# Attention: TensorE's step order from a list schedule made at build time instead of a fixed round

## The chip, the cores and the metric

The kernel runs on one core of a Trainium2 chip. The metric is the device time of one execution in microseconds (us). The kernel computes two transformer-like layers in one launch. The first layer's attention is a stage of its own inside it, and the change touches that stage alone.

## The reference, cut to what matters

The attention stage has 2 batches of 2048 tokens, 16 heads of 16 columns each, a causal mask and a key mask (`T` is 2048 here, `H` 16, `dh` 16):

```python
Qh = Q.reshape(B, T, H, dh)
Kh = K.reshape(B, T, H, dh)
Vh = V.reshape(B, T, H, dh)
scores = jnp.einsum('bqhd,bkhd->bhqk', Qh, Kh) / np.sqrt(dh)
scores = jnp.where(key_mask[:, None, None, :] == 0, NEG, scores)
tril = jnp.tril(jnp.ones((T, T), dtype=scores.dtype))
scores = jnp.where(tril[None, None, :, :] == 0, NEG, scores)
attn = jax.nn.softmax(scores, axis=-1)
attn = attn * query_mask[:, None, :, None]
out = jnp.einsum('bhqk,bkhd->bqhd', attn, Vh).reshape(B, T, U)
```

## The kernel before, in words

`two_layers` runs its stages one behind the other; `attention` is the second. The 32 head-and-batch pairs go through it in 8 head quads of 4 heads (`NQ`, `HQ`). For each quad the softmax is made in two passes. A first pass computes the scores with queries on the partitions, only to find each row's maximum. A second pass computes the scores again, with keys on the partitions and the negated maximum added inside the matmul, so that ScalarE can take the exponential straight away and the values matmul can use it without a transpose.

All engines walk one list, `steps`, made by `plan()` at build time; each takes the entries that concern it, in the order of the list. The kinds are:

- **first** (640, 80 a quad): two matmuls side by side (64x128 tiles, L993) write the scores of two heads for one query tile and up to 512 keys into one of the two slots of `pf`. VectorE reduces them to maxima `mx`: with one TENSOR_REDUCE (L1159) when the block is off the diagonal (48 a quad), with two masked reductions (L1155) when it ends on it (32 a quad). The slot is free after that; `free_slot` waits for it.
- **max** (192): one of six small VectorE steps per block of 512 queries (L1165 to L1177) that split the negated maximum into three bf16 parts, `msp`.
- **rows** (32, one for each quad and query block): TensorE transposes `msp` into a `pf` slot (L999), VectorE copies it to `mT` (L1182), and SyncE sends it by four DMAs (L870) into rows of the operand `qa`. Score steps of that block wait for it (`rows_in`).
- **score** (1152, 144 a quad): for one head, up to 512 queries and one or two key tiles, one or two matmuls (128x128 tiles, L1012), with a mask matmul on the diagonal (L1016), write one of three buffers of `pst` (`NS`). ScalarE takes the exponential into `prob` (L1051) and so frees the buffer.
- **values** (288, 36 a quad): the matmuls of one group for four heads (128x32 tiles, L1028), with `prob` of the group's four exponentials as moving operand. There are three `prob` buffers (`NP`).
- **take** and **turn** (32 each): at the end of a query block VectorE copies `po` to `osb` (L1187), TensorE transposes it into a `pf` slot (L1037), and VectorE divides by the row sums into `att` (L1195 to L1202).

The old `plan()` is a fixed round. For every group it puts four score steps, then the values step of the group `LAG` = 2 groups back, then a turn if one is due. Ahead of each score step it puts as many first steps as keep the first pass `lead(s)` of a quad ahead of the second pass (at most 0.52 of a quad), going by column counts. After each first step it puts one to three max steps, and the rows step comes once six more steps have been listed after the split. It knows no times.

SyncE's queue follows the list too: the rows steps' DMAs, and the loads of quad n+2 (17 DMAs) where the list has quad n's last values step. GpSimd waits for each quad's last values step (L925), stores `att`, and at quad 5 begins sums for the next stage, on which VectorE works (`ahead`) among the scores that follow the last first, max or rows step.

Of the kernel before, what the change touches and what calls it, by code (L numbers as in the profile page):

```python
# [16 lines left out]
P = 128  # L17
# [650 lines left out]
def attention(nc, qs_dram, ks_dram, vs_dram, kbias_dram, mask_dram, att_dram, slots_dram, x_dram, xn_dram, ffn_dram, gamma, x1_dram,  # L668
# [11 lines left out]
    HQ = 4  # L680
    NQ = B * HEADS // HQ
# [6 lines left out]
    W1 = 512  # L688
    NS = 3


    first = []
# [5 lines left out]
    groups = []  # L698
# [7 lines left out]
    NG, N1 = len(groups), len(first)  # L706
    ends = [i for i, f in enumerate(first) if f[2] + f[3] == (f[1] + 1) * P]
    last = [max(g for g in range(NG) if groups[g][0] == qb) for qb in range(NB)]

    LAG, NP = 2, 3
    assert NG % NP == 0
    cost1 = [f[3] + 64 for f in first]
    width = [sum(p[2] for p in g[1]) + 64 for g in groups]
    done_at = [max(i for i, f in enumerate(first) if f[1] // 4 == qb) for qb in range(NB)]

    def lead(s):  # L720
        return min(0.52, 0.21 + 0.6 * s)

    def plan():
        steps, done, spent, passed, chain_, waiting = [], 0, 0.0, 0.0, [], []

        def chain_step():
            if chain_:
                k, m, qb = chain_.pop(0)
                steps.append(("max", m, qb, k))
                if k == 5:  # L730
                    waiting.append((len(steps), m, qb))

        def first_steps(due):
            nonlocal done, spent
            while done < NQ * N1 and spent + cost1[done % N1] / sum(cost1) / 2 <= due:
                m, i = divmod(done, N1)
                steps.append(("first", m, i, 0))
                spent += cost1[i] / sum(cost1)
                done += 1
                chain_step()  # L740
                chain_step()
                if i in done_at:
                    chain_.extend((k, m, done_at.index(i)) for k in range(6))
                    chain_step()

        for j in range(NQ * NG + LAG + 1):
            n, g = divmod(j, NG)
            for hh in range(HQ):
                if n < NQ:
                    first_steps(passed + lead(passed))  # L750
                if waiting and (len(steps) >= waiting[0][0] + 6 or n == NQ):
                    _, m, qb = waiting.pop(0)
                    steps.append(("rows", m, qb, 0))
                if done == NQ * N1:
                    chain_step()
                if n < NQ:
                    steps.append(("score", n, g, hh))
                    passed += width[g] / sum(width) / HQ
            if LAG <= j < NQ * NG + LAG:
                vn, vg = divmod(j - LAG, NG)  # L760
                steps.append(("values", vn, vg, 0))
                if vg in last:
                    steps.append(("take", vn, last.index(vg), 0))
            if j >= LAG + 1:
                tn, tg = divmod(j - LAG - 1, NG)
                if tg in last:
                    steps.append(("turn", tn, last.index(tg), 0))
        assert done == NQ * N1 and not waiting and not chain_
        return steps

    steps = plan()


# [23 lines left out]
    part = sb("c_part", [P, NQB, TT, C // NQB])  # L797
# [1872 lines left out]
def two_layers(nc, x, Wq, bq, Wk, bk, Wv, bv, gamma, beta, Wr, br, W1, b1, W2, b2, w_qkv, w_proj, router_wT, e_bias,  # L2670
# [31 lines left out]
    with ExitStack() as kept:  # L2702
# [3 lines left out]
        with nc.cleanup_on_exit():  # L2706
            with ExitStack() as first:
                shared, load = first_weights(nc, w, beta, C, Wr.shape[1], first)
                with ExitStack() as c:
                    norm_and_project(nc, flat(x), xn, mask, kbias, w, shared, load, QT, qs, ks, vs, ffn, B, T, C, HEADS, HV, c)  # L2710
            with ExitStack() as c:
                attention(nc, rows(qs), rows(ks), vs, kbias, mask, att, slots, flat(x), xn, ffn, gamma, x1, ahead, ahead_r,
                          B, T, C, HEADS, HV, c)
# [79 lines left out]
```

## Time and profile before

| | us |
|---|---|
| median of 3 runs | 2173.13 (2168.01 to 2175.15) |
| profiled execution | 2178.65 |
| its span | 2176.2 |

| engine | busy us | share of the span |
|---|---|---|
| TensorE matmul (PE) | 1814.4 | 83% |
| TensorE weight load (PEld) | 944.1 | 43% |
| VectorE (DVE) | 1514.0 | 70% |
| ScalarE (ACT) | 1031.5 | 47% |
| GpSimd (POOL) | 536.8 | 25% |

The profile is of one execution. A busy time is the sum in which an engine has an instruction under way; matmuls overlap, since the next one streams while the last one drains, so the distance from start to start tells more than the duration. In the rows a timeline line gives the start, the duration of the merged run, the engine, line and operation, and in brackets how long the engine was idle before it and what released it. SPq is the queue on which SyncE issues DMAs.

### The profile page before, as it was taken

What the parts mean: (1) busy time and instruction counts of PE and PEld (TensorE: products, weight loads), DVE (VectorE), ACT (ScalarE), POOL (GpSimd) and SP (SyncE); (2) the same over time, 40 slices, a digit from 0 to 9 for tenths busy, and PEclk for the clock granted to TensorE, in tenths of its full rate; (3) what the DMA queues carried; (4) which work ended last, traced back from release to release, by engine and by line L of the source; (5) the groups of instructions that cost most, each with busy time, mean ns of one, the idle gap of its engine ahead of it and who ended that gap; (6) DMA issues with size and microseconds to landing.
All of it is one profiled execution on the core that took longest, in us unless ns stands there. A gap on an engine that the chain in (4) does not pass through costs nothing. (4 is left out here: it accounts for less than half of the span.)

```text
span 2176.2 us, 34165 instructions
## 1 busy us (share of the span) xinstructions
PE 1814.4 (83%) x11999; PEld 944.1 (43%) x11999; DVE 1514.0 (70%) x3496; ACT 1031.5 (47%) x1908; POOL 536.8 (25%) x592
## 2 busy tenths in 40 slices
PE   0898926899999999999899959799327788999998
PEld 0565602222222222222223236555317555888865
DVE  7987656888888888888788845378206896444456
ACT  3554403466667666666566825356001444323210
POOL 1443350000000000000340000100650786566620
PEclk9999958999999999999999989999658899999999
DMA  3466563013030404040620163000420622566556
GB/s 97 140 212 220 187 157 69 1 25 127 12 140 3 148 2 150 2 150 2 227 79 11 40 230 128 18 2 1 158 85 9 214 95 94 175 188 187 185 198 222
DMA packets 158712, 238.67 MB, mean 110 GB/s; under 512 B 19762, under 2 KB 127282, under 8 KB 156882
## 3 DMA queue, kind: packets, MB, share of 16 engines
q1 hardware_dynamic: 122706, 152.46, 23.0%
q0 software_dynamic: 23136, 75.65, 9.5%
q10 hardware_dynamic: 12704, 8.39, 1.2%
q8 instruction: 99, 1.62, 0.3%
q14 instruction: 67, 0.55, 0.1%
HBM read 116.23 MB, written 119.82 MB: 108 GB/s over the span
## 5 line engine op out<-in xcount | busy, mean ns | idle before, releaser
L1051 ACT ACTIVATE c_prob<-c_pst 128x512 f32<-128x512 f32 (+1 forms) x1152 | 603.1, 573 | 362.3 <-PE c_pst L1012 221.5
L1159 DVE TENSOR_REDUCE c_mx<-c_pf 128x2 f32<-128x1024 f32 x384 | 463.0, 1223 | 92.3 <-PE c_pf L993 89.4
L1012 PE MATMUL c_pst<-c_qa,c_ka 128*128 128x512 bf16 (+3 forms) x1280 | 393.9, 358 | 38.2 <-DMA c_qa<-c_mT 34.6
L993 PE MATMUL c_pf<-c_ka,c_qa 64*128 64x512 bf16 (+3 forms) x1280 | 234.9, 364 | 79.2 <-DVE c_mx L1159 26.4
L1028 PE MATMUL c_po<-c_prob,c_vh 128*32 128x512 f32 (+3 forms) x2560 | 297.2, 547 | 1.5 <-DVE c_osb L1187 0.5
L1155 DVE CUSTOM_DVE_ANT_0 c_spare<-c_pf,c_cut 128x384 f32<-128x384 f32 (+3 forms) x512 | 231.1, 492 | 51.0 <-PE c_pf L993 46.3
L1012 PEld LDWEIGHTS c_pst<-c_qa,c_ka 128*128 128x128 bf16 x1280 | 108.6, 97 | 284.4 <-ACT c_prob L1051 122.7
L993 PEld LDWEIGHTS c_pf<-c_ka,c_qa 64*128 64x128 bf16 x1280 | 61.9, 93 | 313.0 <-issue 126.5
L925 POOL IOTA c_zero<- 128x24 int32 x6 | 1.3, 215 | 697.4 <-PE c_po L1028 697.4
L1980 POOL DMA_INDIRECT s_parts<-x_yr,x_tags x144 | 141.0, 979 | 85.8 <-DVE x_yr L2635 62.4
L2519 PE MATMUL x_ps<-x_gu,x_xs 128*128 x576 | 137.6, 382 | 0.0
L1980 POOL DMA_INDIRECT s_slots<-x_rows,place x128 | 125.8, 983 | 37.9 <-issue 31.3
L2620 DVE TENSOR_TENSOR x_h<-x_ps,x_sg 128x256 f32<-128x256 f32 x72 | 30.6, 424 | 142.4 <-ACT x_sg L2589 123.5
L2067 PE MATMUL i_pm<-i_X,i_AQ 64*64 64x64 f32 x768 | 41.9, 248 | 82.7 <-issue 70.3
L2519 PEld LDWEIGHTS x_ps<-x_gu,x_xs 128*128 128x128 f32 x576 | 105.0, 192 | 11.5
L1016 PE MATMUL c_pst<-c_negk,c_idb 128*128 128x128 bf16 x512 | 95.7, 220 | 0.0
L1028 PEld LDWEIGHTS c_po<-c_prob,c_vh 128*32 128x32 f32 x2560 | 54.6, 109 | 86.4 <-issue 43.2
L2582 ACT COPY x_xs<-x_ps 128x512 f32<-128x512 f32 x72 | 42.2, 587 | 84.5 <-issue 61.3
L2067 PEld LDWEIGHTS i_pm<-i_X,i_AQ 64*64 64x64 f32 x768 | 35.9, 159 | 88.3 <-issue 75.2
L2540 PE MATMUL x_ps<-x_d,x_hT 128*128 x288 | 74.1, 380 | 0.1
L365 POOL TENSOR_TENSOR b_parts<-b_r,b_parts 128x512 bf16<-128x512 f32 x32 | 57.6, 1819 | 57.7 <-ACT b_parts L502 57.7
L2335 ACT ACTIVATE k_e<-k_d 128x1024 f32<-128x1024 f32 x32 | 33.9, 1060 | 74.0 <-POOL k_en L2271 50.5
(383 smaller groups left out, 2934.9 us busy)
## 6 DMA issues: line engine op xcount, KB each, us to landing
s_slots<-c_zero POOLq DMA_DIRECT2D x6, 3264.0 KB, 19.9
x_xr<-s_slots SPq DMA_DIRECT2D x72, 272.0 KB
x_rows<-s_parts SPq DMA_DIRECT2D x8, 2048.0 KB, 8.8
c_qa<-s_qs SPq DMA_DIRECT2D x64, 192.0 KB, 8.3
c_ka<-s_ks SPq DMA_DIRECT2D x64, 192.0 KB, 9.0
s_qs<-b_parts SPq DMA_DIRECT2D x32, 256.0 KB, 2.4
s_ks<-b_parts SPq DMA_DIRECT2D x32, 256.0 KB, 2.7
s_vs<-b_va SPq DMA_DIRECT2D x32, 256.0 KB, 3.8
```

Of the source, the lines that this page charges most:

```text
L365: nc.gpsimd.tensor_tensor(parts[:, i, 2, :], r[:, i, :], parts[:, i, 1, :], ALU.subtract).then_inc(parts_ok, 1)
L993: mm = nc.tensor.matmul(pf[:, slot, h - fh, 0:kn], qa[r, s, h, qt * P:(qt + 1) * P], ka[r, s, h, k0:k0 + kn], start=True, stop=True, tile_ ...
L1012: mm = nc.tensor.matmul(pst[:, u % NS, at:at + qn], ka[:, s, hh, kt * P:(kt + 1) * P], qa[:, s, hh, qb * QB + q0:qb * QB + q0 + qn], start ...
L1016: mm = nc.tensor.matmul(pst[:, u % NS, at:at + P], idb[:], negk[:], start=False, stop=True)
L1028: mm = nc.tensor.matmul(po[HV * h:HV * h + HV, q0:q0 + qn], vh[:, s, kt, h, :], prob[:, a % NP, h, at:at + qn], start=(kt == 0), stop=(a i ...
L1051: nc.scalar.activation(prob[:, g % NP, hh, 0:w], pst[:, u % NS, 0:w], ACT.Exp).then_inc(exp_ok, 1)
L1155: ins = nc.vector.tensor_tensor_reduce(spare[:, h, 0:kn], pf[:, slot, h, 0:kn], cut[:, W1 - kn:], 1.0, 0.0, ALU.add, ALU.max, mx[:, fh + h ...
L1159: nc.vector.tensor_reduce(mx[:, fh:fh + 2, qt, part], pf[:, slot, :, 0:kn], AX.X, ALU.max).then_inc(max_ok, 1)
L1980: return nc.gpsimd.indirect_dma_start(out=dst, out_offset=bass.IndirectOffsetOnAxis(ap=index.bitcast(U32), axis=0), in_=src, in_offset=None)
L2067: mm = nc.tensor.matmul(out[h, s % 2 * NG + g, k, 0:width], lhs(h, n), rhs(h, n), start=True, stop=True, tile_position=(h.start, h.start))
L2519: mm = nc.tensor.matmul(pgu[:, m % 2, i, :], xs[:, m % 2, i, k, :], gu[:, k, bass.ds(e, 1), :].rearrange("p o n -> p (o n)"), start=(k == ...
L2540: mm = nc.tensor.matmul(pyr[:, m % 2, i, :], hT[:, m % 2, i, :], d[:, bass.ds(e, 1), :].rearrange("p o n -> p (o n)"), start=True, stop=True)
```

## The change

`plan()` no longer follows a fixed round. It keeps a clock for TensorE, VectorE and ScalarE, with costs in microseconds for each step, and picks again and again, among the kinds that may come next (first, score, values, rows, turn), the one that can begin earliest. A step of another kind than the one before it begins `SWITCH` = 0.1 later. Each kind has a small bonus or malus (`prefer`). First steps may come only while the first pass is within `lead` of the second, now up to 0.67 of a quad. A score may come only when its rows step is listed and fewer than `NP` groups wait for their values. The steps themselves, their waits and their tiles are the same, and so is all code behind `steps = plan()`.

```diff
--- before.py
+++ after.py
@@ -709,63 +709,130 @@
 
 
 
-    LAG, NP = 2, 3
+    NP, SLOTS = 3, 2
     assert NG % NP == 0
-    cost1 = [f[3] + 64 for f in first]
-    width = [sum(p[2] for p in g[1]) + 64 for g in groups]
+    share1 = [(f[3] + 64) / sum(f[3] + 64 for f in first) for f in first]
+    width = [sum(p[2] for p in g[1]) for g in groups]
+    share2 = [(w + 64) / sum(w + 64 for w in width) / HQ for w in width]
     done_at = [max(i for i, f in enumerate(first) if f[1] // 4 == qb) for qb in range(NB)]
-
-
+    opens = [g for g in range(NG) if g == 0 or groups[g - 1][0] != groups[g][0]]
+
+
+
+    SWITCH, SIGNAL, DRAIN, ROW = 0.1, 0.06, 0.17, 1 / 2400
+    prefer = dict(first=0.11, score=0.0, values=-0.18, rows=0.17, turn=0.29)
 
     def lead(s):
-        return min(0.52, 0.21 + 0.6 * s)
+        return min(0.67, 0.34 + 0.51 * s)
 
     def plan():
-        steps, done, spent, passed, chain_, waiting = [], 0, 0.0, 0.0, [], []
+        steps, chain_, split_, turns = [], [], [], []
+        exp_end, values_end, slot_free, rows_at, taken = [], [], [0.0] * SLOTS, {}, [0.0]
+        pe, shape, act, dve = 0.0, None, 0.0, 0.0
+        firsts = scores = values = 0
+        spent = passed = 0.0
+
+        def start(kind, ready):
+            return max(pe + (SWITCH if kind != shape else 0.0), ready + SIGNAL)
+
+        def issue(kind, ready, stream):
+            nonlocal pe, shape
+            begun = start(kind, ready)
+            pe, shape = begun + stream, kind
+            return pe
+
+        def reduce_at(ready, cost):
+            nonlocal dve
+            dve = max(dve, ready) + cost
+            return dve
 
         def chain_step():
             if chain_:
                 k, m, qb = chain_.pop(0)
                 steps.append(("max", m, qb, k))
+                ready = reduce_at(0.0, 0.19)
                 if k == 5:
-                    waiting.append((len(steps), m, qb))
-
-        def first_steps(due):
-            nonlocal done, spent
-            while done < NQ * N1 and spent + cost1[done % N1] / sum(cost1) / 2 <= due:
-                m, i = divmod(done, N1)
+                    split_.append((ready, m, qb))
+
+        def score_ready():
+            j, hh = divmod(scores, HQ)
+            n, g = divmod(j, NG)
+            if j - values >= NP or (n, groups[g][0]) not in rows_at:
+                return None
+            ready = exp_end[scores - NS] if scores >= NS else 0.0
+            return max(ready, rows_at[n, groups[g][0]]) if hh == 0 and g in opens else ready
+
+        def values_ready():
+            if (values + 1) * HQ > scores or values % NG in last and turns:
+                return None
+            ready = exp_end[(values + 1) * HQ - 1]
+            return max(ready, taken[-1]) if values % NG in opens else ready
+
+        while values < NQ * NG:
+            ready = {"score": score_ready() if scores < NQ * NG * HQ else None, "values": values_ready()}
+            if firsts < NQ * N1 and firsts // N1 <= values // NG + 1 and spent + share1[firsts % N1] / 2 <= passed + lead(passed):
+                ready["first"] = slot_free[-SLOTS]
+            if split_:
+                ready["rows"] = max(split_[0][0], slot_free[-SLOTS])
+            if turns:
+                ready["turn"] = max(turns[0][0], slot_free[-SLOTS])
+            ready = {kind: at for kind, at in ready.items() if at is not None}
+            if not ready:
+                if chain_:
+                    chain_step()
+                    continue
+                ready["first"] = slot_free[-SLOTS]
+            kind = min(ready, key=lambda k: start(k, ready[k]) - prefer[k])
+            at = ready[kind]
+            if kind == "first":
+                m, i = divmod(firsts, N1)
+                fh, qt, k0, kn, part = first[i]
                 steps.append(("first", m, i, 0))
-                spent += cost1[i] / sum(cost1)
-                done += 1
+                end = issue(kind, at, kn * ROW)
+                whole = k0 + kn < (qt + 1) * P
+                slot_free.append(reduce_at(end + DRAIN + 0.043, 1.14 * kn / W1 if whole else 2 * (0.153 + 0.00104 * kn) + 0.02))
+                firsts += 1
+                spent += share1[i]
                 chain_step()
                 chain_step()
                 if i in done_at:
                     chain_.extend((k, m, done_at.index(i)) for k in range(6))
                     chain_step()
-
-        for j in range(NQ * NG + LAG + 1):
-            n, g = divmod(j, NG)
-            for hh in range(HQ):
-                if n < NQ:
-                    first_steps(passed + lead(passed))
-                if waiting and (len(steps) >= waiting[0][0] + 6 or n == NQ):
-                    _, m, qb = waiting.pop(0)
-                    steps.append(("rows", m, qb, 0))
-                if done == NQ * N1:
+            elif kind == "rows":
+                ready_, m, qb = split_.pop(0)
+                steps.append(("rows", m, qb, 0))
+                slot_free.append(reduce_at(issue(kind, at, SIGNAL) + DRAIN, 0.2))
+                rows_at[m, qb] = dve + 7.5
+            elif kind == "turn":
+                ready_, n, a = turns.pop(0)
+                steps.append(("turn", n, a, 0))
+                slot_free.append(reduce_at(issue(kind, at, 0.24) + DRAIN, 1.15))
+            elif kind == "score":
+                if firsts == NQ * N1:
                     chain_step()
-                if n < NQ:
-                    steps.append(("score", n, g, hh))
-                    passed += width[g] / sum(width) / HQ
-            if LAG <= j < NQ * NG + LAG:
-                vn, vg = divmod(j - LAG, NG)
-                steps.append(("values", vn, vg, 0))
-                if vg in last:
-                    steps.append(("take", vn, last.index(vg), 0))
-            if j >= LAG + 1:
-                tn, tg = divmod(j - LAG - 1, NG)
-                if tg in last:
-                    steps.append(("turn", tn, last.index(tg), 0))
-        assert done == NQ * N1 and not waiting and not chain_
+                j, hh = divmod(scores, HQ)
+                n, g = divmod(j, NG)
+                qb, pieces = groups[g]
+                steps.append(("score", n, g, hh))
+                end = issue(kind, at, width[g] * ROW + sum(0.063 if p[0] >= 4 * qb else 0.008 for p in pieces)) + DRAIN + 0.037
+                if hh == 0 and j >= NP:
+                    end = max(end, values_end[j - NP] + SIGNAL)
+                act = max(act, end) + 0.065 + 0.00084 * width[g]
+                exp_end.append(act + 0.1)
+                scores += 1
+                passed += share2[g]
+            else:
+                n, g = divmod(values, NG)
+                steps.append(("values", n, g, 0))
+                values_end.append(issue(kind, at, 4 * width[g] * ROW) + DRAIN)
+                values += 1
+                if g in last:
+                    a = last.index(g)
+                    steps.append(("take", n, a, 0))
+                    taken.append(reduce_at(values_end[-1], 0.6))
+                    turns.append((taken[-1], n, a))
+        steps.extend(("turn", n, a, 0) for ready_, n, a in turns)
+        assert firsts == NQ * N1 and not chain_ and not split_
         return steps
 
     steps = plan()
```

## Rows read from the trace of the kernel before

**Rows 1.** The page, part 1: engine, busy us, share of the span, instructions.
```profile
PE 1814.4 (83%) x11999; PEld 944.1 (43%) x11999; DVE 1514.0 (70%) x3496; ACT 1031.5 (47%) x1908; POOL 536.8 (25%) x592
```

**Rows 2.** Busy us by stretch (instructions): the stage, three steady quads; then granted clock, DMA.
```profile
296.00:1256.00 960.00, 858.29 (x5792) 259.02 (x5791) 796.53 (x1908) 603.11 (x1152) 72.29 (x66) 0.96 0.22 70
706.00:1040.00 334.00, 314.70 (x2173) 96.06 (x2171) 282.62 (x673) 226.09 (x432) 6.54 (x9) 1.00 0.22 74
```

**Rows 3.** Timeline of GpSimd: its IOTA behind quads 0 and 5, the last sum.
```profile
483.19 0.22 POOL L925 IOTA c_zero<- 128x24 int32 x1 [165.09 <-PE c_po L1028]
...
1040.04 0.21 POOL L925 IOTA c_zero<- 128x24 int32 x1 [106.05 <-PE c_po L1028]
...
1118.86 2.36 POOL L945 TENSOR_TENSOR QT<-QT,c_ff 128x1024 f32<-128x1024 f32 x1
```

**Rows 4.** Timeline of TensorE in the steady part, 602 to 606 us.
```profile
602.85 0.64 PE L1028 MATMUL c_po<-c_prob,c_vh 128*32 128x256 f32 x8
603.42 0.39 PE L993 MATMUL c_pf<-c_ka,c_qa 64*128 64x512 bf16 x2
603.74 0.60 PE L1012 MATMUL c_pst<-c_qa,c_ka 128*128 128x512 bf16 x2
604.28 0.39 PE L993 MATMUL c_pf<-c_ka,c_qa 64*128 64x512 bf16 x2
604.60 0.39 PE L1012 MATMUL c_pst<-c_qa,c_ka 128*128 128x512 bf16 x1
```

**Rows 5.** Who waited for whom, 296 to 1256 us: total us, times, longest us.
```profile
PEld c_pf L993 <- DVE c_mx L1159: 101.9, 172, 1.7
...
PE c_pst L1012 <- DMA c_qa<-c_mT: 34.6, 10, 11.3
...
PE c_pf L993 <- DVE c_mx L1159: 26.4, 47, 1.5
```

**Rows 6.** Timeline of TensorE in quad 0: the first two rows steps, and the third score.
```profile
318.74 0.27 PE L999 MATMUL c_pf<-c_idb,c_msp 128*48 128x128 bf16 x1 [0.72 <-DVE c_mx L1159]
324.14 0.59 PE L1012 MATMUL c_pst<-c_qa,c_ka 128*128 128x512 bf16 x1 [5.13 <-DMA c_qa<-c_mT]
...
336.02 0.22 PE L999 MATMUL c_pf<-c_idb,c_msp 128*48 128x128 bf16 x1 [0.18 <-DVE c_mx L1159]
347.57 0.61 PE L1012 MATMUL c_pst<-c_qa,c_ka 128*128 128x512 bf16 x1 [11.34 <-DMA c_qa<-c_mT]
...
384.58 0.61 PE L1012 MATMUL c_pst<-c_qa,c_ka 128*128 128x512 bf16 x1 [5.29 <-DMA c_qa<-c_mT]
```

**Rows 7.** Timelines of SyncE's queue and TensorE at the third rows step of quad 6.
```profile
1039.99 0.32 SPq L851 DMA_DIRECT2D c_qa<-s_qs  x1
...
1050.69 0.43 SPq L861 DMA_DIRECT2D c_vh<-s_vs  x1
1051.17 3.02 SPq L870 DMA_DIRECT2D c_qa<-c_mT  x4
...
1070.70 1.04 PE L1012 MATMUL c_pst<-c_qa,c_ka 128*128 128x512 bf16 x2 [5.77 <-DMA c_qa<-c_mT]
```

**Rows 8.** Timelines of TensorE and ScalarE in the tail, behind the last first step.
```profile
1227.99 0.82 PE L1012 MATMUL c_pst<-c_qa,c_ka 128*128 128x512 bf16 x3
1229.07 0.39 PE L1012 MATMUL c_pst<-c_qa,c_ka 128*128 128x512 bf16 x1 [0.26 <-ACT c_prob L1051]
1229.39 1.07 PE L1028 MATMUL c_po<-c_prob,c_vh 128*32 128x512 f32 x8
1230.39 0.82 PE L1012 MATMUL c_pst<-c_qa,c_ka 128*128 128x512 bf16 x3
...
1228.42 2.07 ACT L1051 ACTIVATE c_prob<-c_pst 128x512 f32<-128x512 f32 x4 [0.33 <-PE c_pst L1012]
```

**Rows 9.** Timeline of VectorE: whole and cut reductions one behind the other.
```profile
1203.03 2.36 DVE L1159 TENSOR_REDUCE c_mx<-c_pf 128x2 f32<-128x1024 f32 x2 [0.37 <-PE c_pf L993]
1205.86 0.69 DVE L1155 CUSTOM_DVE_ANT_0 c_spare<-c_pf,c_cut 128x512 f32<-128x512 f32 x1 [0.46 <-PE c_pf L993]
...
1207.20 0.22 DVE L1165 TENSOR_REDUCE c_nm<-c_mx 128x16 f32<-128x64 f32 x1
```

## The prediction

> **What bounds the kernel now.** I started with busy time by engine [rows 1]: TensorE is busy for 83% of the span, but that is a mean over stages, so the attention stage was cut out next with busy time by stretch [rows 2]. It runs from 296 to 1256 us, 959 us of the profiled 2176.2. In its steady part (706 to 1040 us, three head quads) TensorE is busy 314.7 of 334 us (94%), VectorE 282.6 (85%), ScalarE 226.1 (68%). So TensorE is the bound and VectorE is close behind. The ends of head quads are marked by GpSimd's IOTA, which waits for a quad's last values step [rows 3]: quad 0 ends at 483.2 us and quad 5 at 1040.0, so five quads take 556.8 us, 111.4 each. Before them stand 187 us, behind them 215.
>
> A busy TensorE is not a streaming one. The timeline of its instructions [rows 4] shows what a change of step kind costs. Two score matmuls and then a first step take 0.54 us from start to start (603.74 to 604.28), a first step and then a score 0.32 (603.42 to 603.74). Within a kind a score step costs 0.22: three of them are busy 0.82 us, less 0.39 for the last, over two [rows 8]. So leaving a score step for another kind costs 0.32 in place of 0.22, and leaving a first step 0.32 for 512 columns that stream in 0.21 at the full clock: 0.10 either way. I took the shortest start-to-start distance for each kind, width and successor over all 2144 steps in the trace. The sum for one steady quad is 102.6 us: 75.9 us of columns (77,824 of scores with the masks, 34,816 of firsts, 69,632 of values in four passes, at 2.4 GHz), 1.6 for the turns, 22 for 224 changes of kind, the rest small gaps between matmuls. The quad takes 111.4, so TensorE waits 8.8 us in it. Over the stage the sum is 817 us and the waits 141.
>
> Where the waits are: the waits view [rows 5] gives 34.6 us to "DMA c_qa<-c_mT" in 10 waits, the round trip of the negated row maxima through SyncE's queue; the first two are 5.1 and 11.3 us long and the third, also in quad 0, 5.3 [rows 6]; one of 5.8 comes in quad 6 [rows 7]. The waits on `c_mx` are first steps waiting for one of the two `pf` slots; the view puts 26.4 us on the matmul and 101.9 on its weight load, but the load's idle lies largely beside other matmuls. By the excess over the shortest distances, 58 us are lost in score-to-first steps.
>
> **The change, part by part.** Instructions, shapes, tiles and waits stay as they are: 1152 scores, 640 firsts, 288 values, 32 rows, 32 turns. Only their order changes, for all engines at once, since each walks the same list.
>
> (1) *Changes of kind.* Following the two rules, the old list changes kind 1746 times, the new 1479 times. Scores run in threes (212 such runs in place of 15), a first step stands before a values step 100 times (never before). At 0.097 us each, 267 fewer are 26 us. In a steady quad it is 224 against 191, and the sum falls from 102.6 to 99.4. All of it is on the path while TensorE is the bound, so I take -26.
>
> The Trainium skill (TensorEngine Tiling (Array Packing), Tiling Modes) says that changing the tiling mode drains TensorE. A whole drain would be the 0.39 us that a matmul lasts less its 0.21 of columns, 0.17 us a change and 46 us in all; the distances in rows 4 give 0.10, so the trace sides with less than a whole drain, and the sum goes by it.
>
> (2) *The round trip of the row maxima.* Old list, quad 0: 20 firsts, the rows step, then at once the score that needs its result; TensorE stood still for 5.1 us, then with no step between for 11.3 [rows 6]. New list: the rows step comes after 13 firsts and 9 firsts lie between it and the score; 8 firsts and a turn lie in the second gap, 7 firsts, a values and a turn in the third. These are VectorE-bound at 1.14 us or more each (two reductions busy 2.36 us, one lasting 1.22) [rows 9], so the 8 to 10 us of reductions cover the 5 to 11 us of DMA and are work that must be done anyway. In quad 6 the DMA stood behind 17 loads and landed 19.5 us after its issue began [rows 7]; from quad 3 on the new list puts rows (n,2) ahead of the next quad's loads in SyncE's queue, and the score comes 23 us of work later in place of 16. Of the 34.6 us I leave 8: -26.
>
> (3) *The tail.* After the last first step the old list has 21 groups in the pattern three scores, wait, score, values; a group takes 2.39 us with 0.26 of load idle [rows 8]. ScalarE needs only 4 x 0.49 us (four exponentials busy 2.07, the last lasting 0.60). The new list never puts four scores behind a values step unless it must; at the shortest distances a group is 4 x 0.23 + 0.09 + 1.00 = 2.0 us. 21 x 0.4 is 8, less a little because the tail grows to 24 groups (lead 0.67 in place of 0.52): -7.
>
> (4) *Waits for a `pf` slot.* VectorE's need in a steady quad: 48 whole reductions at 1.14, 32 cut ones of which the widest takes 1.34 [rows 9] and the mean about 1.0, and 12 us of chain, take and turn work: 99 us when counted start to start, 94.2 busy [rows 2]. So at 99.4 TensorE and 99 VectorE the two are level, and a quad can't fall below 99. Lower bound of the effect: nothing of the 58 us, or a loss (the second rival). Upper bound: waits fall to 1 us a quad, 8 x 7.8 = 62 less what (2) and (3) already took, some 45. The new order spaces firsts by 0.9 to 1.6 us around a mean of 1.15 and lets one stand right before a values step of 1.00, so that VectorE has a block queued under it; but pairs of firsts (5 a quad) and the turn, which holds a slot for over 1 us, still collide. I take a quarter, nearer to the lower end because both engines are level: -15.
>
> Nothing else should move. The next quad's loads are needed 36 us of work after they are issued in place of 44, and took under 25. GpSimd's sums for the next stage are done at 1121 us [rows 3], 80 us before VectorE's slices want them; the slices (42 us of VectorE) lie in a tail of some 49. The later stages keep their lines.
>
> Sum: 26 + 26 + 7 + 15 = 74 us. By stretch: quad 0 about -19, the five quads 111.4 to 105.0 (-32), the last two -23. The profiled execution took 2178.65 us (span 2176.2, 2.5 around it), which gives 2104.6; it lay 5.5 above the median of 2173.13, and against the median the forecast is 2099.
>
> **The rivals.** (a) *Only the changes of kind are saved.* The waits move to other places but keep their sum, as VectorE's finishing times set them: -26, with -20 to -45 as its bounds: 2128 to 2153, say 2145. For it: VectorE is at 99 of 111.4 us a quad already. Against it: the first two maxima waits have no cover at all now. 0.20.
> (b) *VectorE keeps its share.* It is 89% occupied by that count, and if its gaps are latencies that no order closes, a quad stays at 111 us and only quad 0 and the tail gain, some 22: 2151. For it: VectorE's order is static too, and a take or turn waits for TensorE in the middle of reductions. 0.05.
> (c) *Slower: the runs of three scores stall.* There are three `pst` buffers; exponentials pass every 0.49 us, scores every 0.22. A run of three that begins before ScalarE has emptied the buffers waits 2 x 0.27 = 0.54 us, with firsts and values queued behind it. 212 runs are 114 us if all do so. It outweighs the 26 us from 48 stalled runs on (if nothing else gains); half of them stalled gives +31, 2204. Against it: in the tail a run of three behind a values step goes through in 0.82 us without a wait [rows 8]. 0.04.
> (d) *More than forecast:* the waits of (4) nearly vanish and quads run at 101: five quads -52 and quads 6 and 7 alike, -105: 2068. 0.11, in which the whole drain of the skill's page, by which (1) would be 46, has 0.02 (2079).
> (e) *The list is new, but the pace is not:* VectorE-bound everywhere and the start unchanged, within 0.3%: 0.03.
>
> **How the numbers follow.** The forecast, 2080 to 2125, has 0.57. The range takes in (a), most of (b) and half of (d): 2074 to 2150. A measurement can tell about 0.3% (6.5 us): faster is 0.57 + 0.20 + 0.05 + 0.11 = 0.93, same 0.03, slower 0.04.
>
> **What would show it.** IOTA marks 105 us apart, the first near 464; the first score near 320 us in place of 324.1; waits on "DMA c_qa<-c_mT" under 10 us; groups of 2.0 us in the tail; VectorE at 90% in the steady part. The forecast fails if exponentials gate the runs of three ("PE c_pst <-ACT c_prob" growing beyond 10 us on the matmul), if marks stay at 108 or more, or if the maxima waits survive behind the loads.

## The result, and the profile after

| | before | after |
|---|---|---|
| median | 2170.57 (2167.47 to 2175.15, 4 runs) | 2087.2 (2080.42 to 2089.88, 4 runs) |
| profiled execution, span | 2178.65, 2176.2 | 2089.54, 2087.8 |
| attention, first step's start to last turn's | 958.3 | 868.7 |

The ratio is 0.961 (95% interval 0.9577 to 0.9642), 83 us less by the medians. The two profiled executions lie 89.1 us apart, and the attention stage is 89.6 us shorter in them, so all of it lies there.

Busy time by stretch (busy us and instructions of PE, PEld, DVE, ACT, POOL; granted clock, DMA share, GB/s) for the whole stage of the changed kernel and for three steady head quads:

```profile
296.00:1168.00 872.00, 828.03 (x5792) 258.10 (x5792) 790.23 (x1908) 579.65 (x1152) 72.77 (x66) 0.96 0.27 78
676.00:979.00 303.00, 301.52 (x2167) 95.40 (x2157) 277.84 (x666) 216.22 (x430) 6.32 (x9) 1.00 0.28 80
```

The answer of before is [rows 2]. Three quads took 334 us and take 303. TensorE is now busy 301.5 of 303 (99.5% in place of 94%), VectorE 277.8, which is 92% in place of 85%. GpSimd's marks behind quads 0 and 5 [rows 3] have moved to 457.58 and 975.45:

```profile
457.58 0.22 POOL L992 IOTA c_zero<- 128x24 int32 x1 [139.09 <-PE c_po L1095]
...
975.45 0.21 POOL L992 IOTA c_zero<- 128x24 int32 x1 [96.34 <-PE c_po L1095]
```

So quad 0 ends 25.6 us earlier and a quad takes 103.6 us on average, 111.4 before. Quad by quad the matmuls' starts give 106.3, 107.3, 101.5, 101.5, 101.4 for quads 1 to 5; quads 3 to 5 are the new steady state. The waits view (total us, times, longest), where [rows 5] had 34.6 us in 10 waits for the maxima's DMA and 26.4 on `c_mx`:

```profile
PE c_pf L1060 <- DVE c_mx L1226: 12.2, 15, 1.5
...
PE c_pst L1079 <- DMA c_qa<-c_mT: 4.8, 2, 2.5
```

The first two round trips of the row maxima now lie under firsts. TensorE's timeline at the second rows step (331.01), to be held against the 11.34 us of [rows 6]:

```profile
331.01 0.22 PE L1066 MATMUL c_pf<-c_idb,c_msp 128*48 128x128 bf16 x1 [0.54 <-DVE c_mx L1226]
332.74 0.63 PE L1104 MATMUL c_pf<-c_idf,c_osb 128*128 128x128 f32 x4 [1.51 <-DVE c_mx L1226]
...
340.79 0.61 PE L1060 MATMUL c_pf<-c_ka,c_qa 64*128 64x512 bf16 x2 [0.74 <-DVE c_mx L1226]
341.33 1.04 PE L1079 MATMUL c_pst<-c_qa,c_ka 128*128 128x512 bf16 x2
```

Ten microseconds pass there too, but a turn and eight firsts are done in them, at VectorE's pace. The tail (TensorE, then ScalarE), against [rows 8]:

```profile
1140.31 0.82 PE L1079 MATMUL c_pst<-c_qa,c_ka 128*128 128x512 bf16 x3
1141.06 1.06 PE L1095 MATMUL c_po<-c_prob,c_vh 128*32 128x512 f32 x8
...
1146.64 2.84 PE L1079 MATMUL c_pst<-c_qa,c_ka 128*128 128x512 bf16 x6 [0.26 <-ACT c_prob L1118]
...
1140.73 1.58 ACT L1118 ACTIVATE c_prob<-c_pst 128x512 f32<-128x512 f32 x3 [0.17 <-PE c_pst L1079]
```

Three scores and a values step take 1.75 us (the next three scores start at 1142.06) with no wait. That is not the time of a group, which has four scores: the list takes scores from a store of finished ones, and now and then a long run fills it up again. The run from 1145.56 on has nine scores; the last six start 0.49 us apart, at ScalarE's pace, and the values step behind them comes 4.85 us after the one before it (1144.56 to 1149.41). From group 20's values step to group 30's it takes 21.6 us (1133.04 to 1154.66), 2.16 a group; before, it took 24.6 (1219.18 to 1243.77), 2.46 a group, with eight of the ten at 2.40.

### The profile page after: what moved, and what is told of

The parts are those of the page before. It is cut to its first block and busy times, and to the rows that moved or that the text cites. A ratio compares the mean times of both kernels' runs of the same rounds, so it can differ in the third digit from the quotient of the medians.

```text
span 2087.8 us, 34165 instructions
## 1 busy us (share of the span) xinstructions
PE 1792.3 (86%) x11999; PEld 946.9 (45%) x11999; DVE 1506.7 (72%) x3496; ACT 1008.5 (48%) x1908; POOL 537.1 (26%) x592
## 5 line engine op out<-in xcount | busy, mean ns | idle before, releaser
L1118 ACT ACTIVATE c_prob<-c_pst 128x512 f32<-128x512 f32 (+1 forms) x1152 | 579.7, 579 | 297.9 <-PE c_pst L1079 173.0
L1079 PE MATMUL c_pst<-c_qa,c_ka 128*128 128x512 bf16 (+3 forms) x1280 | 362.6, 358 | 8.2 <-DMA c_qa<-c_mT 4.8
L1060 PE MATMUL c_pf<-c_ka,c_qa 64*128 64x512 bf16 (+3 forms) x1280 | 230.0, 366 | 47.5 <-DMA c_ka<-s_kbias 22.6
L1079 PEld LDWEIGHTS c_pst<-c_qa,c_ka 128*128 128x128 bf16 x1280 | 110.4, 97 | 203.7 <-ACT c_prob L1118 113.4
L1478 PE MATMUL e_pq<-e_xs,e_w 128*128 128x512 f32 x128 | 61.3, 631 | 9.5 <-ACT QT L1420 9.5
```

The source lines that it names most:

```text
L1060: mm = nc.tensor.matmul(pf[:, slot, h - fh, 0:kn], qa[r, s, h, qt * P:(qt + 1) * P], ka[r, s, h, k0:k0 + kn], start=True, stop=True, tile_ ...
L1079: mm = nc.tensor.matmul(pst[:, u % NS, at:at + qn], ka[:, s, hh, kt * P:(kt + 1) * P], qa[:, s, hh, qb * QB + q0:qb * QB + q0 + qn], start ...
L1118: nc.scalar.activation(prob[:, g % NP, hh, 0:w], pst[:, u % NS, 0:w], ACT.Exp).then_inc(exp_ok, 1)
L1478: mm = nc.tensor.matmul(pq[:, i % 2, :], w[:, k, i * P:(i + 1) * P], xs[:, s, k, :], start=(k == 0), stop=(k == K - 1))
```

## The experiments

Two sums are used below. *Changes* is how often the list changes the kind of TensorE's step. *Shortest sum* is the sum of the shortest start-to-start distances for the list, as in the prediction (816 us for the old list; the 817 there had one rare pair too high). It falls by about 0.1 us for each change fewer, and since rare pairs of steps have few undisturbed examples it is good to a few us only. The stage's time less this sum is its *waits*. Times are rounded one by one.

| kernel | changes | stage us | shortest sum | waits | quad 4 us | ratio to before |
|---|---|---|---|---|---|---|
| before | 1746 | 958.3 | 816 | 142 | 110.9 | 1 |
| changed kernel | 1479 | 868.7 | 790 | 78 | 101.4 | 0.961 |
| e6_old_paired | 1439 | 949.1 | 788 | 161 | 109.9 | 0.9963 |
| e2_vector_free | 1708 | 1043.7 | 811 | 233 | 126.3 | 1.0402 |
| e3_exp_free | 1418 | 906.7 | 785 | 122 | 106.6 | 0.9789 |
| e1_switch_free | 1453 | 971.1 | 788 | 184 | 116.0 | 1.0048 |
| e4_choice_blind | 1500 | 895.5 | 792 | 104 | 104.9 | 0.9763 |
| e10_switch_double | 1248 | 924.2 | 767 | 157 | 110.6 | 0.9875 |
| e9_rows_then_load | 1479 | 862.7 | 790 | 72 | 101.4 | 0.9576 |
| e7_new_start | 1686 | 937.4 | 810 | 127 | 114.9 | 0.9914 |
| e14_blind_rows_then_load | 1500 | 870.6 | 792 | 79 | 103.0 | 0.9588 |
| e15_free_rows_then_load | 1453 | 937.6 | 788 | 150 | 110.9 | 0.9916 |
| e16_old_rows_then_load | 1746 | 941.6 | 816 | 126 | 110.0 | 0.9958 |
| e17_old_lead | 1561 | 918.1 | 799 | 119 | 106.2 | 0.9822 |

The kernel before took 2171 us beside e1, e2, e3 and e6, 2170 beside e4, e7, e9 and e10, and 2121 beside e14 to e17. Those last four ran on another chip, and what was faster there lies behind the attention stage: 864.5 us in e16_old_rows_then_load, 920 in the kernel before. Inside the stage the distances are alike (a values step of 512 columns and then a first step take 0.998 us in both). So across the two chips the stage's times can be compared, and the ratios only roughly, since they have different bases.

The loads that are spoken of below are a head quad's: 21 DMAs, of which 17 are large (192 KB to 1 MB; the 17 of the text above) and 4 have 4 KB each.

**Is it the number of changes, or being ready?** The first edit cuts the changes without any knowledge of times, by listing firsts ahead of heads 0 and 2 only.

```diff
-        return min(0.52, 0.21 + 0.6 * s)
+        return min(0.54, 0.25 + 0.6 * s)
...
-                if n < NQ:
+                if n < NQ and hh % 2 == 0:
                     first_steps(passed + lead(passed))
```

> The old fixed round, but firsts are listed only ahead of heads 0 and 2 of a group, so that scores come in pairs (lead 0.25 + 0.6 s up to 0.54, so that no rows step comes late). 1439 changes of kind, 307 fewer than before and 40 fewer than in the changed kernel, with no knowledge of times. By the count alone: -30 us, 2141, ratio 0.986. By readiness: two firsts one behind the other (92 pairs) and runs of scores wait for VectorE, so half or more of the 30 us comes back as waits: ratio 0.993 to 1.005.

Measured 2163.71 us, ratio 0.9963 (0.9946 to 0.998). The list has fewer changes than the changed kernel and a shortest sum 28 us below that of before; the stage got 9 us shorter. The waits view says where most of the other 19 went:

```profile
PE c_pf L993 <- DVE c_mx L1159: 51.9, 74, 1.5
```

It was 26.4 us before [rows 5] and is 12.2 in the changed kernel; the waits for the maxima's DMA fell by 8 us in this run at the same time. So the number of changes doesn't explain the gain: steps that come when their slot isn't free give the saving back.

**What the plan must know.** One edit hides VectorE from the plan, one hides ScalarE. The first makes the plan think that VectorE is done at once, with a slot as well as with the split maxima and the copied output that a rows step and a turn wait for.

```diff
             dve = max(dve, ready) + cost
-            return dve
+            return ready
```

> The new plan with VectorE taken as never busy: a pf slot is thought free as soon as its matmuls have ended. 1708 changes of kind, 38 fewer than before. By the count alone 0.097 x 38 = 4 us are gained: ratio 0.998. By my theory (waits for slots, 58 us before and 10 after, were closed by the plan's knowledge of VectorE) the slot waits return and a steady quad takes 108 to 112 us; the cover of the first maxima round trips may stay and gives up to 20: ratio 0.988 to 1.0. The rival, that ScalarE's clock in the plan and the covered round trips did it, says 0.97 or below with quads under 105.

Measured 2258.33 us, ratio 1.0402 (1.0366 to 1.0439): slower than before by 4%, outside the range I had given. The waits of first steps for reductions (`c_mx`, on the matmul) are 38.7 us in this run, 43.5 before and 21.5 in the changed kernel. Larger ones came that the old fixed round didn't have. Waits of the whole stage:

```profile
PE c_pf L1066 <- DVE c_msp L1244: 57.7, 31, 5.6
PE c_pf L1104 <- DVE c_osb L1254: 40.8, 32, 2.0
```

The blind plan lists a rows step and a turn right behind VectorE's last step for it, so TensorE stands still 1.9 us for each of 31 rows steps and 1.3 us for each of 32 turns, with all else queued behind it. The old round kept six steps between a split and its rows step. These two lines are 98.5 of the 155 us of waits that this run has above the changed kernel. So it shows that a plan must know when VectorE's results are ready; what knowing the slots alone is worth it doesn't show.

```diff
-                act = max(act, end) + 0.065 + 0.00084 * width[g]
-                exp_end.append(act + 0.1)
+                exp_end.append(end)
```

> The new plan with exponentials taken as free: a pst buffer is thought empty as soon as the score has ended. 1418 changes of kind, 61 fewer than in the changed kernel. By the count alone 2081, ratio 0.958. By rival (c) of the prediction, now with the plan blind to it: 80 runs of four scores in place of 2 and 116 of three stall on the three buffers, 0.5 us or more each: 40 to 60 us back, ratio 0.975 to 0.99, with the waits of TensorE's score matmuls and weight loads on ScalarE grown.

Measured 2122.4 us, ratio 0.9789 (0.9747 to 0.9832), in the range expected. TensorE's matmuls wait for ScalarE:

```profile
PEld c_pst L1078 <- ACT c_prob L1117: 131.6, 319, 0.8
...
PE c_pst L1078 <- ACT c_prob L1117: 14.1, 55, 0.5
```

In the changed kernel the weight load's line reads 113.4 us and the matmul's 0.3. So rival (c) of the prediction is a real mechanism: it comes as soon as the plan doesn't see the exponentials. It stayed small because the plan does. The two lines grew by 18 and 14 us, of 44 us of waits added. Part of the rest is not ScalarE's: this list also has one wait of 6.8 us for the maxima's DMA, behind the loads in quad 6.

**What the 0.1 us for a change of shape does.** First the constant was set to zero, then to double.

```diff
-    SWITCH, SIGNAL, DRAIN, ROW = 0.1, 0.06, 0.17, 1 / 2400
+    SWITCH, SIGNAL, DRAIN, ROW = 0.0, 0.06, 0.17, 1 / 2400
```

> The new plan with SWITCH = 0 in place of 0.1: changes of tile shape are not counted in. Its list changes kind 1453 times, 26 fewer than the changed kernel's 1479. If the gain comes from the number of changes alone (0.097 us each), it is level with the changed kernel: 2087 - 3 = 2084, ratio to before 0.960. If the gain comes from steps being ready when TensorE reaches them, the plan's TensorE clock now runs some 145 us too fast over the stage, steps are placed before they are ready, and waits come back: 5 to 25 us, ratio 0.963 to 0.973.

Measured 2183.27 us, ratio 1.0048 (1.0017 to 1.0079). Both numbers I had written down were wrong: the whole gain is gone, 96 us, although this list has fewer changes than the changed kernel.

```diff
-    SWITCH, SIGNAL, DRAIN, ROW = 0.1, 0.06, 0.17, 1 / 2400
+    SWITCH, SIGNAL, DRAIN, ROW = 0.2, 0.06, 0.17, 1 / 2400
```

> The new plan with SWITCH = 0.2 in place of 0.1. 1248 changes of kind, 231 fewer than in the changed kernel, which is -22 us by the count: 2065, ratio 0.951. The plan's clock now runs some 125 us too slow over the stage. If a right clock is what counts, waits come back, for VectorE's slots above all, since steps come due earlier on the chip than in the plan: 20 to 80 us more waits, so 2085 to 2145, ratio 0.96 to 0.988.

Measured 2142.69 us, ratio 0.9875 (0.9847 to 0.9903), at the upper end of what was expected from a wrong clock. The shortest sum falls by 23 us, as the count says, and the waits grow by 79, with TensorE waiting 124 times for whole reductions in place of 15:

```profile
PE c_pf L1060 <- DVE c_mx L1226: 42.7, 124, 1.5
```

So of the three values tried, the one that is near what the chip takes is the best, by 55 and 96 us. The constant works in two places in the plan, the choice of the next step and TensorE's clock. The next edit takes it out of the choice alone.

```diff
-            kind = min(ready, key=lambda k: start(k, ready[k]) - prefer[k])
+            kind = min(ready, key=lambda k: max(pe, ready[k] + SIGNAL) - prefer[k])
```

> The new plan in which TensorE's clock still adds 0.1 us at a change of kind, but the choice of the next step ignores it. 1500 changes of kind, 21 more than in the changed kernel. If the 0.1 matters because the plan's clock must keep the chip's time, nearly all of the gain stays: 2087 + 2 for the changes, 2085 to 2100, ratio 0.961 to 0.967. If it matters because the choice avoids changes, the result is like that of the plan without SWITCH: 2150 or more, ratio 0.99 or above.

Measured 2117.03 us, ratio 0.9763 (0.9732 to 0.9793): between the two ranges I had given, so neither was right. Its trace has a stall at the same place in each of six quads (here quad 2; the waiting score's own matmul is missing among the records, and the wait is shown at the next one):

```profile
587.73 0.39 PE L1060 MATMUL c_pf<-c_ka,c_qa 64*128 64x512 bf16 x2 [2.29 <-DMA c_qa<-c_mT]
...
572.28 0.47 SPq L928 DMA_DIRECT2D c_vh<-s_vs  x1
572.80 2.97 SPq L937 DMA_DIRECT2D c_qa<-c_mT  x4
```

The four small DMAs of rows (2,2) are issued right behind the DMAs of a load (the last two lines, SyncE's queue) and land only when the loads are through, 15 us later. By the profile the last of the loads lands at 587.24. In the changed kernel that happens in quads 1 and 2 alone; from quad 3 on its rows step (n,2) stands one step ahead of the last values step that releases the load. That is an accident of the list: no line of the plan knows of the queue.

**SyncE's queue.** The load is put behind the rows step (n,2), in the list of the changed kernel.

```diff
+            listed, due = set(), []
...
+                    listed.add((n, a))
...
-                    sp.wait_ge(values_ok, (n + 1) * NG)
-                    load(n + 2, n % 2)
+                    due.append(n)
+                while due and (due[0] + 1, 2) in listed:
+                    m = due.pop(0)
+                    sp.wait_ge(values_ok, (m + 1) * NG)
+                    load(m + 2, m % 2)
```

> The changed kernel with one edit in SyncE's queue: behind quads 0 and 1 the next quad's loads are issued after the rows step (n,2) that follows within 4 us, as the new list has it anyway from quad 2 on. In the changed kernel TensorE waits 2.4 and 2.5 us for these rows (the quads take 106.3 and 107.3 us against 101.5 later). If the queue is the cause, both waits go, and with them the half clock behind them: 2 x 3 to 2 x 5 us less, ratio 0.956 to 0.958, quads 1 and 2 at 101.5 to 103.5. If quads 1 and 2 are longer for their order alone, no change: 0.961.

Measured 2080.16 us, ratio 0.9576 (0.9551 to 0.96), in the range expected and the lowest ratio of all. The interval overlaps that of the changed kernel, so the total doesn't tell the two apart, but the trace does. Quads 1 and 2 take 102.5 and 102.4 us in place of 106.3 and 107.3; the stage gains 6.0 us of these 8.7, since quad 0 took 2.3 us longer in this execution, for a reason not looked into. Busy time by stretch behind the place of the first stall, first the changed kernel, then this one:

```profile
484.00:487.00 3.00, 3.00 (x12) 0.46 (x15) 1.23 (x1) 2.06 (x4) 0.00 (x0) 0.50 0.00 0
```

```profile
484.00:487.00 3.00, 3.00 (x28) 1.04 (x27) 3.00 (x4) 2.08 (x5) 0.00 (x0) 1.00 1.02 232
```

After a wait of 2.37 us TensorE's granted clock is at the lower of its two levels (0.50, 1.2 GHz, the half clock of the expectations) in the changed kernel, and full in the other. That is why waits of 2.4 and 2.5 us cost 4 to 5 us a quad here. It isn't so every time. In e4_choice_blind the five waits of quads 1 to 5 are 2.99, 2.29, 2.73, 2.16 and 2.17 us, and the clock behind them is full, full, lower, full, lower. The stretches behind the third and the fourth:

```profile
693.00:696.00 3.00, 2.76 (x11) 0.70 (x15) 1.51 (x2) 2.17 (x4) 0.00 (x0) 0.50 0.00 0
799.50:802.90 3.40, 3.40 (x29) 1.10 (x30) 2.82 (x6) 2.51 (x5) 0.00 (x0) 1.00 0.00 0
```

The length of the wait alone doesn't settle it: 2.17 us was followed by the lower clock and 2.99 us wasn't.

Now the two uses of the 0.1 us can be parted with the queue out of the way. The first run is e4_choice_blind with the edit in SyncE's queue, the second e1_switch_free with it.

> The plan whose choice ignores the 0.1 us (1500 changes), with the loads of the next quad issued after the rows step (n,2) in every quad. Before that edit it took 2117, 30 us above the changed kernel, and its trace shows a stall of 2.3 to 8.0 us (21 in all) behind the loads in each of six quads, since its list has all six of these rows steps behind the loads and the changed kernel's list only two. If those stalls and the half clock behind them are the difference, it comes to 2080 to 2092, ratio 0.958 to 0.964. If the choice itself costs the time, 2105 or more, ratio 0.97 or above.

Measured 2033.67 us beside 2120.83, ratio 0.9588 (0.9567 to 0.9609), as the queue's explanation said; one wait of 0.7 us for the maxima's DMA is left on the matmul, and quads take 103.0 us. What counting the change of shape in the choice is worth can't be told by the ratios (0.9588 against 0.9576 with the same edit of the queue, from two chips). The stage says that it is something: 870.6 us against 862.7, and 103.0 against 101.5 in a steady quad, 8 us in the two profiled executions, of which the 21 changes are 2.

> The plan with SWITCH = 0, with the same edit in SyncE's queue. Before the edit 2183, 96 us above the changed kernel, with 26 us of stalls behind the loads in six quads. The edit should give back those and the half clock behind them, 26 to 50 us: 2133 to 2157, ratio 0.983 to 0.994. The rest, 50 us or more, is then the price of a plan whose TensorE clock runs too fast (waits for VectorE's slots). If the queue were the whole difference: 2090, ratio 0.963.

Measured 2101.87 us, ratio 0.9916 (0.9896 to 0.9935), in the range of the clock's explanation. This plan and the one before it choose alike, by earliest start without the 0.1 us; they differ in the plan's clock for TensorE alone, and that is 3.3% or 68 us (67 of the stage). The timeline of its quad 4 shows what a fast clock leads to:

```profile
850.70 0.22 PE L1070 MATMUL c_pf<-c_idb,c_msp 128*48 128x128 bf16 x1 [0.56 <-DVE c_mx L1226]
...
853.28 0.61 PE L1064 MATMUL c_pf<-c_ka,c_qa 64*128 64x512 bf16 x2 [0.72 <-DVE c_mx L1226]
...
856.19 0.29 PE L1064 MATMUL c_pf<-c_ka,c_qa 64*128 64x128 bf16 x2 [0.85 <-DVE c_mx L1226]
```

In this plan TensorE is quicker than on the chip, so VectorE looks like the bound, and the firsts fall behind their lead. The last rows step of a quad then comes 8 steps ahead of the score that needs it (32 in the changed kernel), and the plan fills the round trip with seven firsts in a row, each of which waits for a slot; the lower clock follows (matmuls of 0.61 in place of 0.39 us); over the stage the granted clock is 0.92, against 0.97 in e14. That the firsts fall behind for this reason is read from the code and the list, not shown by a run of its own.

> The kernel before with its old list, and only the edit in SyncE's queue. Its waits for the third block's maxima in quads 1 to 6 sum to about 12 us, 5.8 of them in quad 6. They should go, with some half clock: -10 to -16 us, ratio 0.9925 to 0.9955. If this order of the queue were the main part of what the change brought, 0.97 or below.

The same edit on the kernel before: 2108.97 beside 2120.83, ratio 0.9958 (0.9937 to 0.9979), 9 to 12 us. That is at the small end of the range in us and just outside it by the ratio. Behind quad 0 the waits for the maxima's DMA fell from 12.8 to 3.2 us on the matmul. The queue alone is about a tenth of the gain. (The stage is 16.7 us shorter than in the kernel before, but 5.7 of them lie in quad 0, whose queue the edit leaves as it was.)

**The lead and the start.**

```diff
-        return min(0.67, 0.34 + 0.51 * s)
+        return min(0.52, 0.21 + 0.6 * s)
```

> The new plan with the old lead (0.21 + 0.6 s up to 0.52 in place of 0.34 + 0.51 s up to 0.67). 1561 changes of kind, 82 more than in the changed kernel (+8 us). All rows steps (n,2) stand 22 steps behind the loads and so wait for them, six stalls of 2 to 6 us as in the kernel before, +15 to +25; rows steps (n,3) have 19 steps to their score in place of 32. Expected 2105 to 2125, ratio 0.970 to 0.979. If the lead does nothing but the changes it costs: 2095, 0.965.

Measured 2080.59 beside 2120.83, ratio 0.9822 (0.9797 to 0.9846), outside the range of 0.970 to 0.979 that I had given. The stage is 49 us longer than in the changed kernel, so of its gain of 90 us the new lead carries 49 in this list, half and more. Waits for the maxima's DMA are nearly as in [rows 5]:

```profile
PE c_pst L1079 <- DMA c_qa<-c_mT: 31.0, 8, 7.8
```

They are 26 of the 41 us of waits that it has above the changed kernel, and the changes add 9 to the shortest sum. A list by readiness with the old lead still meets the round trip of the maxima unprepared, since the rows steps come late. What the new lead would do to the old fixed round was not run, so the 49 us belong to the lead and the choice by readiness together.

For e7_new_start the two lists were joined: the new one up to quad 0's last values step, and then what is left, in the old order.

> The new list up to the last values step of quad 0, the old list's order for all that is left. 1686 changes of kind. The stretches' gains should stand apart: quad 0 keeps its gain (186.4 to about 160 us), the steady quads go back to 111 each: -27 us, 2144, ratio 0.988. If the start only moves the work and the gain in it is given back, 0.995 or more.

Measured 2153.09 us, ratio 0.9914 (0.9884 to 0.9945), a smaller gain than the 0.988 expected. Quad 0 takes 162.0 us (186.4 before, 159.8 in the changed kernel), and quads 1 to 6 take 111 to 117. The start's gain of 24 us stands nearly by itself: the other quads together give back 3.5 of it. What is left, 21 us, is about a quarter of the whole.

## Why the prediction was right

The forecast was 2099 us and 74 less than before, the result 2087 and 83 less. The path was right: TensorE and VectorE are level, and the gain came from all four terms. The total hides one miss: the terms (1) to (4) were put at 26, 26, 7 and 15, and for the stage's 89.6 us they come out at 26, 30, 6 and 28.

(1) *Changes of kind*, forecast -26: the shortest sum fell from 816 to 790. No run measures this term by itself; it is the count of changes times distances that stayed what they were, and as a steady quad has only about 2 us of waits left, nothing hides it. It isn't a gain that fewer changes bring by themselves: in e6_old_paired the shortest sum is 28 us below that of before, and the stage gained 9. The Trainium skill (TensorEngine Tiling (Array Packing), Tiling Modes) says that a change of mode drains TensorE. The whole drain of 46 us that the prediction estimated from that is not seen in this case: the distance from a first step to a score is still 0.32 us, as in [rows 4].

(2) *The maxima's round trip*, forecast -26: 34.6 to 4.8 us, -30. The firsts covered it at VectorE's pace as worked out, though not for nothing: in quad 0 firsts behind firsts wait 9 us more than before, which (4) has. The rows steps of quads 3 to 7 stand ahead of the loads. The prediction noticed that order; e9 and e14 show that it is worth having on purpose, and e17, with 31.0 us of these waits, that the choice by readiness without the longer lead doesn't bring this term.

(3) *The tail*, forecast -7: the last segment (quad 7) went from 93.4 to 85.0 us, 8.4 less, of which some 6 are waits and the rest is fewer changes, which (1) has. That segment holds more than the tail.

(4) *Waits for a slot*, forecast -15: this was the term that was mis-sized. What is left of the 64 us of waits after (2) and (3) is 28. Score-to-first steps lost 58 us before and 10 now; firsts behind firsts lose 29 where they lost 20, nearly all in quad 0. I had taken a quarter of the 58 "nearer to the lower end because both engines are level". The engines are level, 99.4 and about 99 us of need, and a steady quad takes 101.5, not 105: in this kernel two engines that need the same time were both kept at work with two slots. The forecast's mistake was to expect of level engines that they collide. That it is the plan's knowledge of VectorE that closed these waits is argued from the traces; e2_vector_free, made to show it, was slowed by other waits.

By stretch: quad 0 -26.6 (forecast -19), five quads -39 (-32), the last two -24 (-23).

The rivals: (a), only the changes saved, has no support, as the waits fell by 64 us. (b), VectorE keeps its share, is refuted: its need of 99 us (the 89% of the prediction) now fills 98% of a quad of 101.5, and its busy share went from 85% to 92%. (c), runs of three scores stall, is refuted for this list (scores behind scores lose 14.5 us over the stage, 11.5 before) and supported as a mechanism by e3_exp_free. (d) came nearer than (a): quads 3 to 5 run at the 101 it named, but quads 1 and 2 pay for the queue, and quad 0 is bound by VectorE.

The things named as signs: marks 105 us apart, first near 464 (103.6, first 457.6); first score near 320 us (321.0); waits for the maxima's DMA under 10 us (4.8); groups of 2.0 us in the tail (2.16 on average, so this one was not met; 1.75 is three scores and a values step alone); VectorE at 90% (92%).

What stays open: quad 0 still takes 160 us, with firsts at VectorE's pace and a mean granted clock of 0.84 (296 to 457.5 us); no run tried to shorten it. Its second round trip has the queue in it too: in the kernel before, SyncE issues quad 1's loads from 322.97 to 331.9, the last of them lands at 346.8, the maxima's four DMAs are issued behind them at 337.26, and the score that waits starts at 347.57, the 11.34 us of [rows 6]. The edit of the queue leaves that load where it is, in both lists, and no run moved it. How the loss of e1_switch_free divides between slot waits and lower clock was not parted. Not run either: the new lead in the old round, and the plan without its bonuses (`prefer`).

## What to carry to other kernels

When several engines that work in order share few buffers, an order laid out at build time by real start-to-start durations can bring two engines with the same need to 99% and 92% busy, as here, but its clocks must be right: one constant of 0.1 us, wrong by its own size, turned a gain of 4% into a loss of 0.5% or into 1.2%. Fewer changes or fewer steps are no aim in themselves; ask whether each step finds its buffer free when it is reached. And a plan is only as good as the queues in it: the place of the loads in the DMA queue was worth 6 us in the changed kernel, 25 in e4's list and some 33 in e1's, and how early the rows steps are listed (the lead) was a large part of 49 us.

## What the runs showed of the hardware that I had not expected

A change between the score's, the first's and the values' tile shapes costs 0.10 us from start to start, though a matmul of 512 columns lasts 0.39 us with 0.21 us of columns in it. A wait of 2.4 us on TensorE can be followed by a stretch at the lower clock (0.50 between 484 and 487 us in the changed kernel) and then costs about double; of five waits of 2.2 to 3.0 us in e4_choice_blind two were. Four small DMAs behind a quad's loads in one queue took about 15 us from the first issue to the step that waited for them (572.80 to 587.7 in e4), where quad 0's first round trip took 5.4 us from the rows step to the score [rows 6].
